# Heads in partitions and rows moved by DMA in a softmax attention phase, with four products for maxima behind the values

## The reference

```python
q = (src @ Wq + bq).reshape(B, T, N_HEAD, HEAD_DIM)      # 16 heads of 16
k = (src @ Wk + bk).reshape(B, T, N_HEAD, HEAD_DIM)
v = (src @ Wv + bv).reshape(B, T, N_HEAD, HEAD_DIM)
scores = jnp.einsum('bqhd,bkhd->bhqk', q, k) * HEAD_DIM ** (-0.5)
probs = jax.nn.softmax(scores, axis=-1)
attn = jnp.einsum('bhqk,bkhd->bqhd', probs, v).reshape(B, T, D_MODEL)
x = _layer_norm(src + attn @ Wo + bo, ln1_g, ln1_b)
```

## Time and profile before

| | |
|---|---|
| median of three runs | 2095.5 us (2095.2 to 2095.9) |
| profiled execution | 2098.55 us, span 2096.8 us |
| busy in the span: PE, DVE, ACT, POOL | 89%, 62%, 44%, 47% |
| mean granted clock of PE | 0.954 of full speed |

### The profile page before, as it was taken

How to read it: one execution, slowest core, us unless ns; L and a number is a source line. 1 busy time by engine, 2 the same in 40 slices (tenths; PEclk the granted TensorE clock), 3 DMA queues, 4 the chain that set the end, 5 groups by cost and what they waited for, 6 DMA issues and landing times.

```text
span 2096.8 us, 36970 instructions
## 1 busy us (share of the span) xinstructions
PE 1861.5 (89%) x12145; PEld 1131.9 (54%) x12146; DVE 1308.8 (62%) x2894; ACT 915.6 (44%) x1313; POOL 985.6 (47%) x681
## 2 busy tenths in 40 slices
PE   5999999999998109999479999999999999999998
PEld 3454544544543109999455555646556565554654
DVE  3767677677675416777676565765656666565661
ACT  2657566566566004444225244252432515335152
POOL 2414133242344353544337637385473855738454
PEclk8999999999999659999779999999999999999999
DMA  6300000000002244566400010100101001010000
GB/s 176 131 1 11 10 0 10 10 0 10 0 0 101 91 176 183 213 213 234 114 11 2 11 32 1 42 2 11 32 1 42 2 11 32 1 42 1 15 18 11
DMA packets 56176, 104.86 MB, mean 50 GB/s; under 512 B 7238, under 2 KB 46566, under 8 KB 50156
## 3 DMA queue, kind: packets, MB, share of 16 engines
q1 hardware_dynamic: 52972, 94.71, 13.4%
q0 software_dynamic: 3072, 8.39, 1.2%
HBM read 76.35 MB, written 26.74 MB: 49 GB/s over the span
## 4 chain that ended last, share of the span: by engine, by line
PE 38%; issue 6%; DVE 3%; POOL 2%; ACT 1%; POOLq 0%; DMA 0%; DVEq 0%; ACTq 0%; SPq 0%
PE a_psS L703 10%; PE a_psO L717 10%; PE a_psO L740 6%; PE a_psM L677 5%; PE a_psS L665 4%; PE a_psS L649 2%; PE a_psS L730 1%; POOL a_k_tok L350 1%; ACT a_probs L468 1%; DVE a_junk L534 1%; POOL a_oT L373 1%; POOL a_q_tok L350 1%; DVE a_alibi L611 0%; DVE a_qL L524 0%; DVE a_rden L548 0%
## 5 line engine op out<-in xcount | busy, mean ns | idle before, releaser
L385 POOL TENSOR_TENSOR a_probs<-a_probs 128x1024 f32<-128x1024 f32 x144 | 340.8, 2393 | 315.9 <-PE a_psO L717 315.9
L534 DVE CUSTOM_DVE_ANT_0 a_junk<-a_psM,a_alibi 128x512 bf16<-128x512 f32 x512 | 333.7, 689 | 215.0 <-PE a_psM L677 214.1
L1282 DVE TENSOR_REDUCE f_q_tok<-f_psR 128x1 f32<-128x512 f32 x512 | 323.2, 682 | 136.6 <-PE f_psR L1437 136.0
L468 ACT ACTIVATE a_probs<-a_psS 128x1024 f32<-128x1024 f32 x256 | 248.8, 1024 | 284.0 <-PE a_psS L703 283.9
L1220 ACT ACTIVATE f_probs<-f_psS 128x1024 f32<-128x1024 f32 x256 | 248.3, 1025 | 64.0 <-PE f_psS L1456 63.4
L717 PE MATMUL a_psO<-a_probs,a_v 128*32 128x512 f32 x2048 | 244.0, 597 | 0.0
L1437 PE MATMUL f_psR<-f_kP,f_qM 64*128 64x512 f32 x512 | 161.3, 498 | 25.6 <-DVE f_q_tok L1282 17.9
L677 PE MATMUL a_psM<-a_kH,a_qH 64*128 64x512 f32 x512 | 126.3, 488 | 34.0 <-DVE a_n_tok L534 29.0
L1469 PE MATMUL f_psO<-f_probs,f_v 128*32 128x512 f32 x1024 | 136.4, 604 | 0.7 <-ACT f_probs L1220 0.6
L740 PE MATMUL a_psO<-a_wo,a_oT 128*128 128x256 f32 x512 | 131.2, 404 | 4.4 <-POOL a_oT L373 4.4
L1843 ACT ACTIVATE e_h<-e_psH,w_o 128x256 f32<-128x256 f32 x152 | 63.8, 471 | 148.7 <-PE e_psH L1935 148.7
(11 more groups left out here) (201 smaller groups left out, 3783.3 us busy)
## 6 DMA issues: line engine op xcount, KB each, us to landing
w_w_high<-w_parts SPq DMA_DIRECT2D x19, 1024.0 KB, 5.5
w_w_low<-w_parts SPq DMA_DIRECT2D x19, 1024.0 KB, 7.6
sorted_x<-f_zeros SPq DMA_DIRECT2D x1, 4864.0 KB, 21.2
e_xs<-sorted_x SPq DMA_DIRECT2D x19, 256.0 KB, 2.7
sorted_z<-e_z SPq DMA_DIRECT2D x19, 256.0 KB, 2.2
f_xn<-in_L_attn_x SPq DMA_DIRECT2D x8, 512.0 KB, 3.5
f_w_raw<-in_L_ffn_W SPq DMA_DIRECT2D x4, 1024.0 KB, 9.2
w_parts<-f_w_high SPq DMA_DIRECT2D x4, 1024.0 KB, 3.9
```

What stands on the lines that cost most here:

```text
L385: nc.gpsimd.tensor_tensor(slots, slots, probs[:, first - GRP:first - GRP + 2, :], ALU.add).then_inc(added.sem, 1)
L468: nc.scalar.activation(probs[:, slots, :], psS[:, 2 * p:2 * p + 2, :], ACT.Exp).then_inc(exp_done.sem, 1)
L534: nc.vector.tensor_tensor_reduce(out=junk[:, a, :], in0=psM[:, a, :], in1=alibi[:, h, :], scale=1.0, scalar=-3.0e38, op0=ALU.add, op1=ALU.max,
L1282: nc.vector.tensor_reduce(q_tok[:, c, h, NEG:NEG + 1], psR[:, ring_bank("max", u), :], AX.X, ALU.max, negate=True).then_inc(max_done.sem, 1)
```

## The change

Projections now have the weights as the stationary operand, so that q and k come out with heads in partitions and tokens along the row: four "sides" (keys and queries, for pairs 0 to 3 and 4 to 7). ACT writes each side twice from PSUM (whole, rounded), POOL subtracts. Then SP moves the three parts of each side into the pairs' layout: 12 DMAs for each half of the pairs, each from 64 partitions into 16, 128 KB. All turns of keys and queries go. The maxima of a quad are turned as 128x4 columns into 4 rows, copied by ACT and moved by two small DMAs into a row of `qP`, which both products and scores read. All four products of a period stand behind the values, the extras behind them, then the turns. The clearing of `sorted_x`, preloads and W1 come later in SP's order, and so does the second split of W1 in POOL's.

```diff
-    AHEAD = MQ + 2
+    AHEAD = 2 * (MQ + 4)
-              (1, 2): [("proj", 0)], (1, 3): [("proj", 1)], (2, 0): [("proj", 2)], (2, 1): [("proj", 3)],
+              (1, 0): [("proj", 0)], (1, 1): [("proj", 1)], (1, 2): [("proj", 2)], (1, 3): [("proj", 3)],
+    TURNED = {(0, 2): [("maxima", 1, 0)], (0, 3): [("rows", 0, 0), ("rows", 1, 2)], (1, 2): [("maxima", 2, 0)],
+              (2, 2): [("maxima", 3, 0)], (3, 2): [("maxima", 0, 0)]}
     def maxima(r):
+        first = (AHEAD + 4 * r) % (2 * QUADS * MQ)
+        return [], [first, first + 1, first + 2, first + 3]
...
+            def move_sides(b, g):
+                if not (isinstance(b, int) and b == 0):
+                    sp.wait_ge(score_ps.sem, score_ps.at(b - 1, QP * (2 * g + 2) * TT - 1))
+                for i, (pair_rows, kinds) in enumerate(((kP, (high, low, high)), (qP, (high, high, low)))):
+                    n = 2 * g + i
+                    sp.wait_ge(low_done.sem, low_done.at(b, n))
+                    for a in range(2):
+                        for k, part in enumerate(kinds):
+                            first = FB * a + FH * k
+                            sp.dma_start(pair_rows[first:first + FH, HP * g:HP * (g + 1), :].bitcast(F32),
+                                         part[FB * a:FB * (a + 1), n, :].bitcast(F32)).then_inc(moved[g].sem, 16)
...
+            move_sides(0, 0)
+            load_rows(0)
+            move_maxima(0, 0)
+            move_sides(0, 1)
+            sp.dma_start(sorted_x.rearrange("(n p) d -> p n d", p=P),
+                         zeros[:, :].unsqueeze(1).to_broadcast([P, TILES * TOK // P, D])).then_inc(cleared, 16)
+            for tile, source in preloads:
+                sp.dma_start(tile, source).then_inc(preloaded, 16)
+            def batch(b, more, last):
+                move_maxima(b, 1)
+                move_maxima(b, 2)
+                if more:
+                    if not last:
+                        load_rows(b + 1)
+                    move_sides(b + 1, 0)
+                move_maxima(b, 3)
+                if more:
+                    move_maxima(b + 1, 0)
+                    move_sides(b + 1, 1)
+            load_w1(0)
+            batch(0, True, False)
+            for e in range(NE // 2):
+                store_w1(e)
+                load_w1(e + 1)
...
                 if before:
                     finish_rows(b - 1)
+                for e in splits[1:]:
+                    split_w1(e)
...
+                if j == 0 and p == 0:
+                    pe.wait_ge(n_moved.sem, n_moved.at(b, quad))
...
+                    for u in late:
+                        if present(b, "max", u):
+                            multiply_for_max(b, u)
+                    for kind, n in EXTRAS.get(divmod(r, TT), ()):
...
+                    for kind, n, bank in turned:
+                        pe.wait_ge(exp_done.sem, exp_done.at(b, QP * r + bank // QP))
+                        transpose(b, kind, n, bank)
```

More of the change, by code:

```diff
@@ L863, in belongs @@
+    def maxima(r):
+        first = (AHEAD + 4 * r) % (2 * QUADS * MQ)
+        return [], [first, first + 1, first + 2, first + 3]
     def belongs(kind, n):
-        return {"max": int(n < 2 * AHEAD), "v": 1 - n, "proj": 1, "out": -1, "rows": 1, "keys": int(n < 4),
-                "queries": int(n < 4), "shifted": int(n < 2)}[kind]
+        return {"max": int(n < AHEAD), "v": 1 - n, "proj": 1, "out": -1, "rows": 1, "maxima": int(n == 0)}[kind]
     def present(b, kind, n):
@@ L1007, in load_w1, with move_maxima @@
+            def move_maxima(b, quad):
+                sp.wait_ge(n_row_done.sem, n_row_done.at(b, quad))
+                for a in range(2):
+                    row = FB * a + NEG
+                    sp.dma_start(qP[row:row + 1, QP * quad:QP * (quad + 1), :].bitcast(F32),
+                                 n_row[QP * a:QP * (a + 1), quad % 2, :].bitcast(F32)).then_inc(n_moved.sem, 16)
             def load_w1(e):
@@ L1194, in high_last @@
-            def high_last(b):
-                src = qk[:, :, FH * LAST:D].rearrange("p t (h d) -> p t h d", d=FH)
-                for a in range(2):
-                    first = 2 * FH * a
-                    last = nc.scalar.copy(q_tok[:, :, LAST:, first:first + FH].bitcast(F32R), src)
-                last.then_inc(hi_last.sem, 1)
-            def take(b, kind, n, bank):
-                batch = b + belongs(kind, n)
-                produced = {"keys": kT_ps, "queries": qM_ps, "shifted": qS_ps, "rows": xnT_ps}[kind]
-                out = {"keys": lambda: kP[:, n, :], "queries": lambda: qM[:, n % 2, :],
-                       "shifted": lambda: qS[:, n % 4, :], "rows": lambda: xnT[:, n, :]}[kind]()
-                act.wait_ge(produced.sem, produced.at(batch, n))
-                nc.scalar.copy(out, psS[:, bank, :]).then_inc(taken[kind].sem, 1)
+            for c in range(KC):
+                for i in range(2):
+                    for g in range(2):
+                        columns = raw[:, c, i, 2 * FB * g:2 * FB * (g + 1)].rearrange("p (e a d) -> p a d e", e=HP, a=2)
+                        nc.scalar.mul(wqk[:, c, 2 * g + i, :].rearrange("p (a d e) -> p a d e", a=2, d=FH), columns,
+                                      FH ** -0.5 if i else 1.0).then_inc(scaled, 1)
@@ new lines, in take @@
+            def take(b, kind, n, bank, first=False):
+                batch = b + belongs(kind, n)
+                if kind == "rows":
+                    act.wait_ge(xnT_ps.sem, xnT_ps.at(batch, n))
+                    nc.scalar.copy(xnT[:, n, :], psS[:, bank, :]).then_inc(xnT_sb.sem, 1)
+                    return
+                if not first:
+                    act.wait_ge(n_moved.sem, n_moved.at(batch, n - 2))
+                act.wait_ge(nT_ps.sem, nT_ps.at(batch, n))
+                nc.scalar.copy(n_row[:, n % 2, :], psS[0:4, bank, :]).then_inc(n_row_done.sem, 1)
@@ L1228, in batch @@
                     for kind, n, bank in turned_in(b, r):
-                        take(b, kind, n, bank)
+                        take(b, kind, n, bank, not before and n == 1)
                     if j == 0:
@@ L1303, in add_rows, with batch @@
                 nc.vector.tensor_tensor(r1[:, t, :], xnb[:, t, :], bank[:, 0:D], ALU.add).then_inc(r1_done.sem, 1)
-            def periods(b, which, before, more):
-                for r in which:
+            def batch(b, before, more):
+                for r in range(PERIODS):
                     quad, j = divmod(r, TT)
@@ L1481, in batch @@
                     for p in range(QP):
-                        scores(b, r, p)
+                        scores(b, r, p, before)
                     if r:
@@ L1521, in _ @@
+            pe.wait_ge(xnT_sb.sem, xnT_sb.at(0, 0))
+            transpose(-1, "maxima", 0, 0)
             project(-1, "v", 0)
+            pe.wait_ge(n_row_done.sem, n_row_done.at(0, 0))
             pe.wait_ge(wo_in, 4 * 16)
```

350 lines of the change are left out of this document (135 added, 215 removed).

## The result

The changed kernel takes 2230.6 us (median of four runs, 2222.7 to 2238.3) against 2095.4 beside it: a ratio of 1.065 (95% interval 1.060 to 1.069), slower by 135 us. I had forecast 2186, with a range to 2225. The direction and PE's waits came as forecast, the size did not. Its profiled execution has a span of 2233.2 us against 2096.8.

What follows compares the result with a forecast made beforehand. PE's program order with its waits for DVE was taken as the bound. Six batches gave 52.8 us, single waits 33.0, with the first and last batch +90 together: 2186 us for a run, range 2120 to 2225.

Steps and rivals of the forecast that it cites:

- Light period: PE's period without turn or extra, values to values: 3.17 us, sixteen per steady batch, 50.7 us.
- extras: Projection or values behind product 4 start 0.60 us after it, waiting for a bank; six singles 14.0, two output pairs 8.2.
- turn to scores: After a turn of maxima PE waits for ACT's copy before the next scores: 1.51 us, four per batch, 6.0.
- DVE's lateness: Statistics and inverted sums delay reductions in (0,1), (2,1), (3,0), (3,1): together 5.9 us a batch.
- The moves: Twelve 128 KB transfers per half take 14.4 us; 2.9 late in (2,2) of seven batches, on time in (0,2).
- Once: Costs that fall once in the program, at its start, in batches 0 and 1 and at the end: 33.0 us.
- Start: Before the first product, copies, POOL and moves add 6.1 us; 3.9 is regained by the first scores, net +2.2.
- (b): Batch 0's maxima of quad 1 queue in SP behind the clearing of sorted_x: +10.8 us; second half of moves 2.5 more.
- (c): POOL's second split of W1 stands before the normalizing that batch 1's output rows need: +12.5 us.
- (d): In the last batch a split on POOL stands ahead of the last normalizing: the end moves by about 5 us.
- The clock: Only in rival "Slower still", chance 0.10, from 2225 us up: long pauses lower PE's clock, adding up to 14 us.
- The moves at the issue's pace: Rival, chance 0.29: moves land as fast as SP issues them, on time in (2,2); sum +47, 2143 us.

Runs made afterwards that it cites:

- e2: Changed kernel with two products between scores and values and two behind the values, instead of four together; 2156.5 us, ratio 1.030.
- e3: Changed kernel with turns directly behind the values, ahead of the four products; 2184.5 us, ratio 1.042.
- e1: Changed kernel with one unread matmul of 256 columns ahead of each fourth product, half filling PE's short pause; 2211.0 us, ratio 1.056.
- e13: Changed kernel with unread matmuls cut to fit nearly all of PE's pauses, nothing moved or left out; 2200.1 us, ratio 1.047.
- e4: Changed kernel with products two and two around the values and turns directly behind the values; 2122.8 us, ratio 1.012.
- e6: On e4, the queries' six moves issued on ACT's queue from batch 1 on, SP keeping the keys'; 2121.2 us.
- e7: On e4, moves by quads: 24 of 64 KB, the first quad's twelve first with their own signal; 2083.4 us, ratio 0.995.

## Why the prediction was wrong in size

Step by step, in the changed kernel's profiled execution:

- *Light period, extras, turns.* 3.17 forecast, 3.18 measured; extra 0.60 behind product 4, as forecast; turn to scores 1.51 forecast, 1.27 measured. e2 and e3 removed most of these and got 74 and 46 us, what the clock gave back included: shown.
- *DVE's lateness.* In (2,1) 0.97 forecast on top of the 0.55, 0.85 measured (1.40). In (0,1) 2.83 and 2.69 (3.24), in (3,0) 1.17 and 1.07 (1.62).
- *The moves.* Forecast 14.4 us for twelve and 2.9 late in (2,2); measured 1.16 to 2.9, 10.6 us in five waits. (0,2) and the small DMAs behind the moves, which I had called on time, were, but for 0.59 us once.
- *Once.* Start: first product forecast 42.7, measured 43.48, and the first scores 2.3 us later than before, forecast 2.2; (b) 10.8 and 8.85, with 2.5 and 1.3 for the second half; (c) 12.5 and 6.55; (d) about 5, and PE's last wait for POOL is 8.8 against 3.8: 5.0. Together 33.0 forecast and 24.0 measured.
- *The clock*, the step that failed. The prediction put it only among the rivals: "the pauses of 3.5 us in (0,1) or of 10 us in (b) and (c) let the clock fall to 1.2 GHz", "the first adds up to 14 us". The sum itself had it at nothing. It fell in every batch, at two or three places, and behind pauses of 1.2 to 3.2 us: 8.1 us a steady batch (96.9 less 88.8), and 42.6 over the phase. e1 showed the sign, e13 the size. With this term the sum is 90 + 43 = 133; measured are 135. That they agree to 2 us is in part luck: the single waits were 9 us too dear in the sum, and in e13, where PE comes earlier, (c) is 11.4 instead of 6.55, so the 42.6 are what is left after that.
- *A rival's sum.* The moves at the issue's pace give +49 by its own terms, not +47; nothing hangs on it.

By batches, each from one values' projection of (0,1) to the next: 98.8 and 102.7 us for the first two, where (b) and (c) fall, then 387.7 for four and 95.0 for the last. Before, they took 75.0, 80.5, 322.1 and 79.7.

Why did I size the clock wrongly? The earlier trace rows has a clock of 1.00 with PE busy for 75.7 of 80 us, and I looked for pauses that were long. But the new order has a pause in every period, three or four of them longer in each batch, and PE's work had shrunk besides: the phase went from 92% busy (554.13 of 600) to 80%. The Trainium skill ("TensorE: Matmul & The Clock Gate", "A second HAM failure mode: psum-queue depth-cycling") describes this kind of case: a kernel that cycles through PSUM banks idles for very short times between groups of matmuls, often enough that the clock swings between its two levels. By that, the three banks of psR were the sign to read. This case's windows agree in part: the clock swings, with 0.50 at 340 to 352 and values between the levels on either side. But the shortest bank waits, 0.55 us in each period, stand in windows of 1.00, and it fell behind the longer ones, where DVE or a move was late. No run fills only the one or only the other kind.

Of the moves' pace the Trainium skill ("SBUF — State Buffer", "Door 1: The DMA port swizzle") gives 104 GB/s for partitions 0 to 15, measured at 1 MiB. Here 122 were measured in e4's window and 142 to 144 for its other half, so the measurement decides. e6 shows that the queue doesn't set the pace; that the number of partitions does was not tried. At 122 GB/s 128 KB take 1.07 us and at 144 0.91, both below the 1.2 that I took.

## What to carry to other kernels

With three banks, four dependent products in a row make one round trip of the reducing engine visible in every period; spread them, and put the turn whose copy must come back ahead of work that can hide it. When an edit takes work from PE without taking its waits, price the granted clock too: it cost 43 us here beside the pauses themselves. Look for the places in a batch where a pause grows beyond the regular one, since the low stretches stood behind those. A resource counts for more once the waits ahead of it are gone: when the moves land is worth 3.6 us a steady batch on the changed kernel and 6.4 with spread products. And compare the phase as well as the whole program: here the untouched rest differed by up to 34 us between traces.

## What the runs showed of the hardware

- In the changed kernel's trace the granted clock falls to 0.50 behind pauses of 1.2 to 3.2 us (1.40 and 1.16, 1.62, 3.24 in one batch), although PE is busy for 80% of the phase, and stays at 1.00 where the pauses are 0.55 to 0.66; one added matmul in each period brought it from 0.85 to 0.92 and the program from 2231 to 2211 us.
- A plain float32 matmul of 384 columns is two instructions, 0.91 us at full clock; I had taken 0.37, and the filled pause of 0.55 became a delay of 0.22 in each light period (3.18 to 3.40).
- Moves of 128 KB between SBUF partitions with 16 destination partitions ran at 122 to 124 GB/s in all for most of one half of the pairs and at 142 to 144 for the other in e4, with the DMA engines full; a second queue changed nothing in e6. Moves of 64 KB ran at 98 to 111 GB/s in e7, one issue every 0.63 us, with the engines less than half busy.
